# Splitting fp32 weights into high and low parts: staged through four slots and PSUM copies, or loaded at once into the low parts' own places

## The reference

```python
x0 = emb[ids].reshape(ids.shape[0], -1)            # 2048 x 1664
x = x0
for i in range(3):
    s = x @ cross_w[i]
    x = x0 * s[:, None] + cross_b[i] + x
h = relu(x0 @ w1 + b1)                             # 1664 -> 1024
h = relu(h @ w2 + b2)                              # 1024 -> 512
h = relu(h @ w3 + b3)                              # 512 -> 256
logit = concatenate([x, h], axis=1) @ out_w + out_b
return sigmoid(logit)
```

## Time and profile before

| what | us |
|---|---|
| median of 3 runs (lowest, highest) | 551.85 (551.65, 551.87) |
| the profiled execution | 551.13 |
| its span, first to last instruction | 549.3 |
| PE matmul busy | 472.4 |
| POOL busy (416 gathers) | 399.4 |
| DVE busy | 147.9 |
| ACT busy | 112.6 |

### The profile page before, as it was taken

How to read it: one execution, slowest core, us unless ns; L and a number is a source line. 1 busy time by engine, 2 the same in 40 slices (tenths; PEclk the granted TensorE clock), 3 DMA queues, 4 the chain that set the end, 5 groups by cost and what they waited for, 6 DMA issues and landing times.

```text
span 549.3 us, 6933 instructions
## 1 busy us (share of the span) xinstructions
PE 472.4 (86%) x2875; PEld 438.1 (80%) x2875; DVE 147.9 (27%) x311; ACT 112.6 (20%) x241; POOL 399.4 (73%) x423
## 2 busy tenths in 40 slices
PE   0075028999999999999999999999999999999997
PEld 0075027989898998989898989989898989898896
DVE  2563123222222213131222222121313222222214
ACT  4894321110111101111111111111111111111101
POOL 5777777777777777777777777777777777777740
PEclk9999558999999999999999999999999999999999
DMA  7848999998898988888888888887868676576610
GB/s 184 192 134 211 97 63 21 24 26 23 26 23 26 25 24 26 24 26 22 26 25 24 28 22 26 24 26 24 25 23 25 25 24 26 24 24 26 22 8 2
DMA packets 18113, 23.00 MB, mean 42 GB/s; under 512 B 8303, under 2 KB 9554, under 8 KB 18082
## 3 DMA queue, kind: packets, MB, share of 16 engines
q0 software_dynamic: 13312, 11.77, 72.1%
q1 hardware_dynamic: 4496, 10.71, 5.6%
q10 hardware_dynamic: 274, 0.08, 0.1%
HBM read 24.41 MB, written 0.01 MB: 44 GB/s over the span
## 4 chain that ended last, share of the span: by engine, by line
POOL 70%; issue 23%; PE 5%; DMA 1%; DVE 0%; POOLq 0%; ACT 0%; DVEq 0%
POOL stage L249 29%; POOL x_raw L249 28%; POOL x_raw L246 8%; POOL stage L246 5%; PE l_bank L565 3%; PE l_bank L635 1%; DMA stage<-in_L_rec_emb,idx 1%; DMA ids<-in_r_ids 0%; PE h_bank L565 0%; POOLq L82 0%; PE x_bank L578 0%; PE x_bank L604 0%; PE h_bank L604 0%; DVE stage L440 0%; DVE stage L438 0%
## 5 line engine op out<-in xcount | busy, mean ns | idle before, releaser
L249 POOL DMA_INDIRECT stage<-in_L_rec_emb,idx x171 | 161.5, 945 | 52.1 <-issue 52.1
L249 POOL DMA_INDIRECT x_raw<-in_L_rec_emb,idx x162 | 153.7, 949 | 51.8 <-issue 49.1
L565 PE MATMUL l_bank<-w_hi,xT_hi 128*128 128x342 f32 (+1 forms) x624 | 146.3, 334 | 36.4 <-DVE xT_lo L400 36.3
L565 PE MATMUL l_bank<-w_lo,xT_hi 128*128 128x342 f32 (+1 forms) x624 | 138.7, 322 | 0.0
L565 PE MATMUL l_bank<-w_hi,xT_lo 128*128 128x342 f32 (+1 forms) x624 | 138.7, 322 | 0.0
L565 PEld LDWEIGHTS l_bank<-w_hi,xT_hi 128*128 128x128 f32 x624 | 103.3, 191 | 43.7 <-DVE xT_lo L400 41.8
L565 PEld LDWEIGHTS l_bank<-w_hi,xT_lo 128*128 128x128 f32 x624 | 107.3, 191 | 0.0
L565 PEld LDWEIGHTS l_bank<-w_lo,xT_hi 128*128 128x128 f32 x624 | 107.1, 191 | 0.0
L400 DVE TENSOR_TENSOR xT_lo<-x_bank,xT_hi 128x512 fp32r<-128x512 f32 (+3 forms) x66 | 38.1, 578 | 201.1 <-ACT xT_hi L293 201.1
L293 ACT ACTIVATE xT_hi<-x_bank 128x512 fp32r<-128x512 f32 (+3 forms) x66 | 33.4, 506 | 262.6 <-PE x_bank L578 262.6
L565 PE MATMUL l_bank<-w_hi,h1T_hi 128*128 128x512 f32 x120 | 50.9, 424 | 12.8 <-DVE h1T_lo L405 12.8
(11 more groups left out here) (81 smaller groups left out, 359.5 us busy)
## 6 DMA issues: line engine op xcount, KB each, us to landing
stage<-in_L_rec_w SPq DMA_DIRECT2D x18, 512.0 KB, 7.1
x_raw<-in_L_rec_emb,idx POOLq DMA_INDIRECT x208, 6.3
stage<-in_L_rec_emb,idx POOLq DMA_INDIRECT x208, 6.1
b_rows<-in_L_rec_b SPq DMA_DIRECT2D x1, 512.0 KB, 5.2
b_rows<-in_L_rec_b SPq DMA_DIRECT2D x1, 256.0 KB, 5.8
ids<-in_r_ids SPq DMA_DIRECT2D x1, 208.0 KB, 2.6
b_rows<-in_L_rec_b SPq DMA_DIRECT2D x1, 128.0 KB, 5.8
out_w_rows<-in_L_rec_out_w SPq DMA_DIRECT2D x1, 128.0 KB, 5.8
```

What stands on the lines that cost most here:

```text
L249: pool.indirect_dma_start(out=dst, out_offset=None, in_=emb, in_offset=rows).then_inc(landed, 16)
L565: done = pe.matmul(bank[:, 0:b - a], x[:, k, :], w[:, k, a:b], start=(k == 0 and n == 0), stop=(k == last_k and n == 2))
```

## The change

The slots, their waits on SP and the copies in PSUM go. Each of the 18 loads has a place and a semaphore of its own: the place is that of its low part (`w1_raw` and `w1_lo` have the same addresses, likewise `w2`, `w3`). SP issues all 18 with no wait between them, save that the bias rows stand behind the 13th as before. ACT makes `hi` with one instruction per load. DVE then subtracts in place, `lo = raw - hi`, with one instruction of 1024 columns per load, both inputs and the output in SBUF. `h1`, `h2`, `h3` and the second gather buffer are tensors of their own.

The order of the work changes with it. ACT's fills for tile 0 and the cross columns stood ahead of the first split; now the cross columns stand behind split 0 and all seven fills (tiles 0 and 1) behind split 1. The last three splits (two pairs of `w2`, and `w3`) move behind `h1` of tile 0 on ACT and on DVE, and PE waits for them in `l2` and `l3` of tile 0 rather than ahead of `transpose_h1`.

```diff
+    WIDTH = N1
+    W2K, W3K = WIDTH // N2, WIDTH // N3
...
-    SLOTS = 4
...
-    SPLITS = [range(0, 6), range(6, 10), range(10, 13), range(13, len(LOADS))]
+    SPLITS = [range(0, 6), range(6, 10), range(10, 13), range(13, 15)]
+    LATE = range(15, len(LOADS))
...
-        stage = sb("stage", [P, SLOTS, STAGE])
-
-        h1, h2, h3 = stage[:, 2, :], stage[:, 3, 0:N2], stage[:, 3, N2:N2 + N3]
...
+        with nc.sbuf_tensor("w1_raw", [P, K1, W1C], F32) as w1_raw, nc.sbuf_tensor("w2_raw", [P, K2, N2], F32) as w2_raw, \
+                nc.sbuf_tensor("w3_raw", [P, K3, N3], F32) as w3_raw:
+            pass
+        w1_lo, w2_lo, w3_lo = sb("w1_lo", [P, K1, W1C], F32R), sb("w2_lo", [P, K2, N2], F32R), sb("w3_lo", [P, K3, N3], F32R)
+        w1_hi, w2_hi, w3_hi = sb("w1_hi", [P, K1, W1C], F32R), sb("w2_hi", [P, K2, N2], F32R), sb("w3_hi", [P, K3, N3], F32R)
+        h1, h2, h3 = sb("h1", [P, N1]), sb("h2", [P, N2]), sb("h3", [P, N3])
...
-        x_buf = [x_raw[:, :], stage[:, 0:2, :].rearrange("p s c -> p (s c)")]
+        x_buf = [sb(f"x_raw{b}", [P, D]) for b in range(2)]
...
-        HI_BANK = [l2_bank, h_bank[1], h_bank[0]]
...
+        def parts(n):
+
+            name, k, m = LOADS[n]
+            of = {"w1": (w1_raw, w1_hi, w1_lo), "w2": (w2_raw, w2_hi, w2_lo), "w3": (w3_raw, w3_hi, w3_lo)}[name]
+            return [w[:, k:k + m, 0:WIDTH // m] for w in of]
...
-                if BEFORE[n] is not None:
-                    sync.wait_ge(weights_split, 2 * (BEFORE[n] + 1))
-                    sync.wait_ge(hi_split, BEFORE[n] + 1)
-                src = {"w1": w1, "w2": w2, "w3": w3}[name][k * P:(k + m) * P, :]
-                dst = stage[:, SLOT[n], :]
-                if m > 1:
-                    src = src.rearrange("(m p) c -> p m c", m=m)
-                    dst = dst.rearrange("p (m c) -> p m c", m=m)
-                sync.dma_start(dst, src).then_inc(stage_loaded[SLOT[n]], 16)
+                src = {"w1": w1, "w2": w2, "w3": w3}[name][k * P:(k + m) * P, :].rearrange("(m p) c -> p m c", m=m)
+                sync.dma_start(parts(n)[0], src).then_inc(weights_loaded[n], 16)
...
             def split_hi(n):
-                name, k, m = LOADS[n]
-                act.wait_ge(stage_loaded[SLOT[n]], 16 * USE[n])
-                dst = {"w1": w1_hi, "w2": w2_hi, "w3": w3_hi}[name][:, k:k + m, 0:STAGE // m]
-                src = stage[:, SLOT[n], :].rearrange("p (m c) -> p m c", m=m)
-                act.activation(dst, src, ACT.Copy).then_inc(hi_split, 1)
-                act.wait_ge(hi_split, n + 1)
-                for i, cols in halves(n):
-                    if i >= len(HI_BANK):
-                        act.wait_ge(weights_split, i - len(HI_BANK) + 1)
-                    bank = HI_BANK[i % len(HI_BANK)][:, 0:HALF]
-                    if m == 1:
-                        hi = dst[:, 0, cols]
-                    else:
-                        hi, bank = dst[:, (i % 2) * m // 2:(i % 2 + 1) * m // 2, :], bank.rearrange("p (m c) -> p m c", m=m // 2)
-                    act.activation(bank, hi.bitcast(F32), ACT.Copy).then_inc(hi_staged, 1)
+                raw, hi, _ = parts(n)
+                act.wait_ge(weights_loaded[n], 16)
+                act.activation(hi, raw, ACT.Copy).then_inc(hi_split, 1)
 
...
-                        if n == FREED[1]:
-                            act.wait_ge(weights_split, 2 * (FREED[0] + 1))
-                            fill(1, 0)
-                            fill(1, 1)
-                            act.wait_ge(weights_split, 2 * (FREED[1] + 1))
-                            fill(1, 2)
-                            fill(1, 3)
+                        if n == 0:
+                            cross_hi()
+                        if n == 1:
+                            fills()
                     x_hi(0, g)
                 h1_hi(0)
+                for n in LATE:
+                    split_hi(n)
 
             def step(t):
                 x_hi(t, 0)
...
-            act.wait_ge(end_row_loaded, 16)
-            for g in range(1, NG):
-                fill(0, g)
-            act.wait_ge(vecs_transposed, 1)
-            act.activation(vec_cols[:, :], h_bank[0][:, 0:VR], ACT.Copy).then_inc(vec_cols_ready, 1)
-            act.wait_ge(vec_cols_ready, 1)
-            act.activation(w1_hi[:, :, N1:W1C], vec_cols[:, 0:VECS * K1].rearrange("p (v k) -> p k v", v=VECS),
-                           ACT.Copy).then_inc(cross_hi_ready, 1)
+            def cross_hi():
+                act.wait_ge(vecs_transposed, 1)
+                act.activation(vec_cols[:, :], h_bank[0][:, 0:VR], ACT.Copy).then_inc(vec_cols_ready, 1)
+                act.wait_ge(vec_cols_ready, 1)
+                act.activation(w1_hi[:, :, N1:W1C], vec_cols[:, 0:VECS * K1].rearrange("p (v k) -> p k v", v=VECS),
+                               ACT.Copy).then_inc(cross_hi_ready, 1)
+
+            def fills():
+                act.wait_ge(end_row_loaded, 16)
+                for t in range(2):
+                    for g in range(NG):
+                        if t > 0 or g > 0:
+                            fill(t, g)
...
             def split_lo(n):
-                name, k, m = LOADS[n]
-                lo = {"w1": w1_lo, "w2": w2_lo, "w3": w3_lo}[name]
-                for i, cols in halves(n):
-                    dve.wait_ge(hi_staged, i + 1)
-                    bank = HI_BANK[i % len(HI_BANK)][:, 0:HALF]
-                    if m == 1:
-                        dst, src = lo[:, k, cols], stage[:, SLOT[n], cols]
-                    else:
-
-                        first = k + (i % 2) * m // 2
-                        dst, width = lo[:, first:first + m // 2, 0:STAGE // m], STAGE // m
-                        src = stage[:, SLOT[n], cols].rearrange("p (m c) -> p m c", c=width)
-                        bank = bank.rearrange("p (m c) -> p m c", c=width)
-                    dve.tensor_tensor(dst, src, bank, ALU.subtract).then_inc(weights_split, 1)
+                raw, hi, lo = parts(n)
+                dve.wait_ge(hi_split, n + 1)
+                dve.tensor_tensor(lo, raw, hi.bitcast(F32), ALU.subtract).then_inc(weights_split, 1)
...
-                dve.wait_ge(weights_split, 2 * len(LOADS))
-                dve.wait_ge(hi_split, len(LOADS))
                 l1_out(0)
                 dots_out(0)
                 h1_lo(0)
+                for n in LATE:
+                    split_lo(n)
...
-                        pe.wait_ge(weights_split, 2 * (k + 1))
-                        pe.wait_ge(hi_split, k + 1)
+                        pe.wait_ge(weights_split, k + 1)
...
+                if t == 0:
+                    last = LOADS.index(("w2", ks[-1] // W2K * W2K, W2K))
+                    pe.wait_ge(weights_split, last + 1)
...
             def l3(t, halves=1):
+                if t == 0:
+                    pe.wait_ge(weights_split, len(LOADS))
...
-                pe.wait_ge(weights_split, 2 * len(LOADS))
-                pe.wait_ge(hi_split, len(LOADS))
```

More of the change, by code:

```diff
@@ L59, in dcn_ranker_kernel @@
     assert N1 % P == 0 and N2 == 4 * P and N3 <= 512 and NG % 2 == 0 and HB * P <= 512
-    STAGE = N1
-    W2K, W3K = STAGE // N2, STAGE // N3
+    WIDTH = N1
+    W2K, W3K = WIDTH // N2, WIDTH // N3
     LOADS = [("w1", k, 1) for k in range(K1)]
@@ L66, in dcn_ranker_kernel @@
     LOADS += [("w3", k, W3K) for k in range(0, K3, W3K)]
-    SLOTS = 4
[L70 to L73, removed]
-    SPLITS = [range(0, 6), range(6, 10), range(10, 13), range(13, len(LOADS))]
-    assert GROUPS[1][-1] * P + P == STAGE and FREED == [max(n for n in range(len(LOADS)) if SLOT[n] == i) for i in range(2)]
+    SPLITS = [range(0, 6), range(6, 10), range(10, 13), range(13, 15)]
+    LATE = range(15, len(LOADS))
     assert all(GROUPS[g][-1] < SPLITS[g].stop for g in range(NG))
@@ L90, in sem @@
             return ctx.enter_context(nc.semaphore(name))
-        w1_hi, w1_lo = sb("w1_hi", [P, K1, W1C], F32R), sb("w1_lo", [P, K1, W1C], F32R)
-        w2_hi, w2_lo = sb("w2_hi", [P, K2, N2], F32R), sb("w2_lo", [P, K2, N2], F32R)
-        w3_hi, w3_lo = sb("w3_hi", [P, K3, N3], F32R), sb("w3_lo", [P, K3, N3], F32R)
-        stage = sb("stage", [P, SLOTS, STAGE])
-        h1, h2, h3 = stage[:, 2, :], stage[:, 3, 0:N2], stage[:, 3, N2:N2 + N3]
+        with nc.sbuf_tensor("w1_raw", [P, K1, W1C], F32) as w1_raw, nc.sbuf_tensor("w2_raw", [P, K2, N2], F32) as w2_raw, \
[4 more added lines that the diff above has]
+        h1, h2, h3 = sb("h1", [P, N1]), sb("h2", [P, N2]), sb("h3", [P, N3])
         b1_rows, b2_rows, b3_rows = sb("b1_rows", [P, N1]), sb("b2_rows", [P, N2]), sb("b3_rows", [P, N3])
@@ L102, in dcn_ranker_kernel @@
         out_b_rows = sb("out_b_rows", [P, 1])
-        x_raw = sb("x_raw", [P, D])
-        assert 2 * STAGE >= D
-        x_buf = [x_raw[:, :], stage[:, 0:2, :].rearrange("p s c -> p (s c)")]
+        x_buf = [sb(f"x_raw{b}", [P, D]) for b in range(2)]
         xT_hi, xT_lo = sb("xT_hi", [P, K1, P], F32R), sb("xT_lo", [P, K1, P], F32R)
```

(13 more changed lines are left out.)

## The result

The changed kernel takes 558.13 us (median of 4 runs, 557.28 to 559.71) against 551.83 us for the kernel before: 6.3 us or 1.05% slower, ratio 1.0105 with a 95% interval of 1.0073 to 1.0137. The forecast was 559.2, range 554.3 to 568.0.

The account below looks back on a forecast made before the run. POOL, full with back-to-back gathers, was taken as the bound. Gathers held by 7 single subtractions (2.9 us) and 3 runs (4.4) gave 7.3 us, other parts 0; on the 551.85 median that made 559.2 us, range 554.3 to 568.0.

Parts of the forecast that it names:

- POOL is the bound, PE's stall is repaid: Over the whole span: POOL's back-to-back gathers set the end; PE catches up by tile 15, so removing its stall saves 0.
- Slots, SP's waits, fills, loads at once: 0 each: At the start: dropping slots and waits, moving fills behind two splits and issuing 18 loads at once each cost 0.
- The price of a hold: A gather starting inside a two-SBUF-input DVE instruction waits until 0.12 us before its end; 0.41 us per single subtraction, 1.46 per run.
- The length of one subtraction: On DVE: one subtraction of 1024 columns with both inputs in SBUF takes 1.23 us.
- The count: Of 18 subtractions, 7 single at 0.41 us and 11 in runs of 4, 4 and 3 at 1.46 per run: 7.3 us.
- No turn inside a run: Rival, 0.14: a gather is held through a whole run of subtractions, 13.7 us in all, so 565.6 us.
- They cost POOL nothing: Rival, 0.09: the subtractions hold no gathers, start-up holds might be a cold queue; 551.9 us.
- PE as the bound: Rival, 0.05: PE was the bound at the end, at `transpose_x(15, 1)`, so its early stall is time won; 550.2 us.
- loads beyond the cover: Rival, 0.06: loads beside the gathers fill POOL's queue or make the fills late, 4 us on top of 7.3; 563 us.
- The Trainium skill: Cited for two-SBUF-input instructions blocking GpSimd reads; its inferred remark that `tensor_tensor` doesn't stop descriptor writing would mean no change.
- The clock staying at full: Sign in the profile after: PE opens tile 1 at 60 us or earlier, then waits briefly for gathers, its clock still full.
- None longer anywhere else than before: Sign in the profile after: gathers up to 2 us beside the 18 subtractions, and no longer gathers elsewhere than before.

Follow-up runs that it names:

- the doubled dose: The changed kernel plus, behind each subtraction, a second DVE instruction of 1024 columns with two SBUF inputs and unused output; 568.67 us, ratio 1.0274.
- the part run alone: The kernel before, slots kept, with only the copies in PSUM gone and one subtraction per load straight from SBUF; 559.49 us, ratio 1.0116.
- the PSUM copies: The changed kernel with hi copied to PSUM again and each load subtracted in two instructions with one PSUM input; 552.63 us, ratio 1.0005.
- 18 copies: Kernel with PSUM copies, finer last tile, h3 and clamped indices in PSUM (549.13 us), plus an unused SBUF-to-SBUF fp32 DVE copy behind each load's subtractions; 552.48 us.
- its variant with only the finer last tile: The kernel before with only the last tile's groups cut as 4, 3, 2, 1, 1, 1, 1 instead of 4, 4, 2, 1, 1, 1; 550.10 us, ratio 0.9964.
- the four kernels profiled there: On the slower chip (kernel before 780.29 us): PSUM copies back 776.01, SBUF subtraction alone with slots 765.59, subtractions cut in two 770.32, second subtraction added 772.55 us.

## Why the prediction was right

- *POOL is the bound, PE's stall is repaid.* Right. With the stall gone and no holds the time is that of before (ratio 1.0005), and in the changed kernel PE opens tile 1 34.6 us earlier for nothing.
- *Slots, SP's waits, fills, loads at once: 0 each.* Their sum is 0 within what the runs can tell; the parts were not run one by one. The fills began at 9.5 us, 0.2 later than before, the ninth gather waited for none.
- *The price of a hold.* Right: "held until 0.12 us before that one's end". For a gather that starts 0.10 us in, the text has 1.05 us in one place, while its own rule gives 1.11 - 0.10 = 1.01. The profile has 0.99 for just that case, and 0.96 to 1.04 deep in runs.
- *The length of one subtraction.* Right: 1.23 us forecast, 1.221 measured.
- *The count.* 7.3 us were forecast; ten gathers were held for some 6.5, and POOL's busy time grew by 6.9 with L440's share. The grouping was not as I had it: four pairs (splits 0 and 1, 2 and 3, 4 and 5, 13 and 14), one run of four (6 to 9) and two of three (10 to 12, 15 to 17), and none alone. The pairs cost 0.99, 0.13, 0.43 and 0.04 us, 1.6 together, where I had 3.1 for these eight subtractions; the three runs cost 1.72, 1.37 and 1.81, 4.9 together, where I had 4.15. That the two errors partly cancel is luck: how much a pair costs hangs on when the gathers happen to start.
- *The rivals.* "No turn inside a run" is refuted by the run of four from 29.14 to 33.77, in which two gathers were issued, and by the doubled dose. "They cost POOL nothing" is refuted by the ten held gathers and by the part run alone. PE as the bound (550.2) and loads beyond the cover (563) fall with the PSUM copies, at 552.63 us, and the fills came on time.
- *The Trainium skill.* Its page "SBUF — State Buffer", section "Who interferes with whom", has a remark that descriptor writing isn't stopped by `tensor_tensor`. The forecast set this against the holds. The two may both be so: the gather reads `idx` in SBUF, and it is held only at its start, while a subtraction that begins later adds 0.1 us at most. No run here separates the reading from the writing. The rule of the same page of the Trainium skill on two SBUF inputs, and its rule that fp32 copies take both shared ports, agree with the runs (0.99 us for one subtraction, 3.35 us for 18 copies).
- *What I had wrong in the list of signs.* "The clock staying at full": the profile's mean is 0.988, with a mean of 0.84 from 70 to 80 us. PE waits for gathers after that stretch, so I count no cost. "None longer anywhere else than before": L402 held gathers up to 1.20 us long, against 1.07.

## What to carry to other kernels

Where POOL issues gathers back to back it can be the bound though its busy share (73% here) is below PE's. In this kernel each gather that started inside a DVE instruction with two SBUF inputs added the rest of that instruction, less some 0.12 us, to the total. Price such an instruction by its own length, and try one operand in PSUM. Before crediting a removed stall, follow the stalled engine to the point where it next waits for something that the change doesn't move. Sum the held time in the profile and compare it with the difference of the medians; if they agree, as here within 0.6 us, take that part of the change out alone to confirm it.

## What the runs showed of the hardware that I had not expected

- An fp32 copy within SBUF, one input, holds gathers too, and also some that have already begun (3.35 us for 18 copies of 0.69 us).
- Gathers landed in 6.1 to 6.4 us at the median in the kernel before and its variant with only the finer last tile, and in 4.3 to 4.5 in every other kernel on the usual chips, also with the slots kept. What the first two have in common is that PE runs late: behind the first tile PE waits for no gather before 520 us in the kernel before and before 435 in its variant. The landings shorten as PE catches up: in the kernel before they took 8.4 and 8.8 us at the median for gathers issued from 60 to 130 us (one figure for each buffer), 6.4 and 6.1 from 270 to 340, and 4.6 and 4.0 from 410 to 480. The gathers' packets took 72% of the DMA engines' time over the whole span against some 60%. Why is open.
- On one chip the same program took 780 instead of 552 us. In the four kernels profiled there POOL waited for ACT's fills; the first cause is open.
